# Scores of the second attention from two f16 halves of the context, which the first stage stores

## The reference, cut to what matters

```python
x = x + _L0_xattn_ref(ctx_1024, _layernorm(x), w_q, w_kv, w_out, b_out)      # 16 heads, keys and values from the context
x = x + _L0_ffn_ref(_layernorm(x), gate_w, gate_b, expert_w, expert_b)       # all 8 experts, weighted by counts
x = x + _L1_xattn_ref(_layernorm(x), ctx_1024, ctx_1024, mask)               # one head, context as keys and values
x = x + _L1_ffn_ref(_layernorm(x), W1, b1, W2, b2, Wg, bg)                   # the best 2 of 8 experts a token

def _L1_xattn_ref(q, k, v, mask):
    logits = jnp.einsum('bqd,bkd->bqk', q, k) * scale
    logits = logits + mask * NEG
    attn = jax.nn.softmax(logits, axis=-1)
    return jnp.einsum('bqk,bkd->bqd', attn, v)
```

## Time and profile before

| | us |
|---|---|
| median of three timed runs | 1064.37 (1064.32 to 1065.72) |
| profiled execution, its own time | 1060.8 |
| profiled execution, span from first to last instruction | 1059.0 |
| TensorE busy | 959.3 (91%) |
| VectorE busy | 763.2 (72%) |
| ScalarE busy | 552.9 (52%) |
| GpSimd busy | 564.6 (53%) |
| mean granted clock of TensorE, of full speed | 0.97 |

### The profile page before, as it was taken

The page is one execution under the profiler, slowest core; times in us unless marked ns, Lnnn a source line. Parts: engine busy times, 40 slices in busy tenths (PEclk is TensorE's granted clock), DMA queues, the critical chain, the costliest instruction groups (busy, mean ns, idle before and its releaser), DMA issues. The chain is left out here.

```text
span 1059.0 us, 31414 instructions
## 1 busy us (share of the span) xinstructions
PE 959.3 (91%) x10666; PEld 675.3 (64%) x10666; DVE 763.2 (72%) x2164; ACT 552.9 (52%) x1090; POOL 564.6 (53%) x904
## 2 busy tenths in 40 slices
PE   4799999999999999988799999999963699999993
PEld 2466666666666666656456666666642588888872
DVE  4688788887888888894768888888765266666553
ACT  3566666666666666655224444444442355555541
POOL 6655454555545555410126777777776355555444
PEclk9999999999999999998799999999997799999997
DMA  5644344444444344322355656555561355555443
GB/s 153 174 136 135 104 121 122 136 110 123 118 127 136 110 122 120 108 79 83 104 151 166 187 189 194 181 179 184 182 197 58 119 91 90 98 96 92 83 63 41
DMA packets 104687, 134.03 MB, mean 127 GB/s; under 512 B 23713, under 2 KB 93873, under 8 KB 104369
## 3 DMA queue, kind: packets, MB, share of 16 engines
q1 hardware_dynamic: 90994, 113.93, 36.6%
q0 software_dynamic: 13536, 18.10, 10.1%
HBM read 93.80 MB, written 38.73 MB: 125 GB/s over the span
## 5 line engine op out<-in xcount | busy, mean ns | idle before, releaser
L991 DVE TENSOR_REDUCE smax<-psum 112x2 f32<-112x750 f32 x240 | 221.2, 934 | 45.8 <-PE psum L443 44.5
L823 ACT ACTIVATE probsT<-psum 125x896 f32<-125x896 f32 x173 | 158.8, 918 | 54.7 <-PE psum L458 53.4
L1963 POOL DMA_INDIRECT out_dram<-y,token_at x70 | 111.9, 1599 | 112.0 <-DMA out_dram<-y,token_at 53.5
L2044 ACT ACTIVATE h<-psum,b 128x256 f32<-128x256 f32 x140 | 58.7, 470 | 99.5 <-PE psum L1991 99.5
L1718 DVE SCALAR_TENSOR_TENSOR acc<-psum,neg_bias,acc 128x448 f32<-128x448 f32 x112 | 75.8, 679 | 10.8 <-PE psum L1542 10.7
L443 PE MATMUL psum<-k_stack,q_stack 63*128 63x375 f16 x480 | 78.5, 326 | 3.5 <-DVE smax L991 0.7
L478 PE MATMUL psum<-probsT,v_aug 125*32 125x112 f32 x2688 | 81.6, 262 | 0.0
L1461 POOL DMA_INDIRECT dispatch_dram<-rows,slots_at x64 | 64.0, 1000 | 28.4 <-issue 28.4
L1542 PE MATMUL psum<-xT_hi,we_hi 128*128 128x448 f16 x256 | 70.2, 356 | 1.1 <-ACT we_hi L1640 1.1
L396 POOL CAST k_hi<-we 128x375 f16<-128x375 f32 x64 | 31.9, 498 | 73.6 <-ACT we L843 73.5
L458 PE MATMUL psum<-q_stack,k_stack 64*128 64x112 f16 x1384 | 64.2, 212 | 7.3 <-DMA q_stack<-neg_max 2.7
(11 more groups left out here) (277 smaller groups left out, 2455.6 us busy)
## 6 DMA issues: line engine op xcount, KB each, us to landing
k_stack<-k_hi_dram SPq DMA_DIRECT2D x64, 188.0 KB, 2.8
we<-in_ctxT_dram SPq DMA_DIRECT2D x32, 375.0 KB, 3.7
ctxT<-in_ctxT_dram SPq DMA_DIRECT2D x32, 375.0 KB
ctx_rows<-in_ctx_dram SPq DMA_DIRECT2D x32, 375.0 KB
rows_e<-dispatch_dram SPq DMA_DIRECT2D x70, 136.0 KB, 2.4
w_raw<-in_w_dram SPq DMA_DIRECT2D x32, 256.0 KB, 3.8
k_hi_dram<-k_hi SPq DMA_DIRECT2D x32, 188.0 KB, 3.2
k_lo_dram<-k_lo SPq DMA_DIRECT2D x32, 188.0 KB, 3.4
```

What stands on the lines that cost most here:

```text
L823: nc.scalar.activation(probsT[:, p, c, hg, :, :, :].rearrange("p k h q -> p k (h q)"), psum[0:KC, 0:2, 0:4 * S], ACT.Exp, scale=float(HD) ...
L991: nc.vector.reduce_max(smax[:, (u - LAG_B) % 2, 2 * (s % 4) + s // 4::PAIRS], psum[0:S, pair_bank(s):pair_bank(s) + 2, 0:KV], AX.X).then_i ...
L1963: nc.gpsimd.indirect_dma_start(dram["out"], bass.IndirectOffsetOnAxis(token_at[:, n % 2, s:s + 1], 0), y[:, n % 2, s, :], None, compute_op ...
L2044: nc.scalar.activation(h[:, c, :], psum[:, 1 + c // 2, (c % 2) * TILE:(c % 2 + 1) * TILE], ACT.Relu, bias=b1[:, c, bass.ds(e, 1)]).then_in ...
```

## The change

In the first stage SyncE gets `halves_out(b)`: two transfers that store `ctx_hi` and `ctx_lo` of batch b, 187.5 KB each, in a new tensor in device memory. It is called in step b behind the queries' rows into `q_stack` and ahead of the load or `q_hi` out; in step 2 it isn't called, and in step 3 for the batches 2 and 3. Two semaphores, `ctx_out0` and `ctx_out1`, count the stores of even and odd batches. `ctx_high` and `ctx_low` wait for those of the batch two before, whose slot they write, and SyncE for all of them before the next weights are loaded.

In the second stage the f32 load of the context becomes one load of both halves, of as many bytes. `x2nT` becomes `x2nT_hi`, by ScalarE ahead of the row normalisation instead of behind it, and `x2nT_lo`, a new subtraction on VectorE ahead of mixture 3. The scores are six f16 products instead of two f32 ones, and TensorE waits for `x2nT_lo` ahead of the last two. The turning of x3 moves from ahead of the ranks to behind them. Left out of the diff below: to make room for three new semaphores, `share_ps` is merged with `share_rdy`, `route_split` with `bias_rdy` and `pads_out` with `late_in`, each with its counts raised.

```diff
@@ -178,6 +178,7 @@
...
     MASK_AT = 2 * UNROLL
+    LATE_HALVES = 2
 
@@ -238,6 +239,13 @@
         @block.sync
         def _(sp):
+            def halves_out(b):
+
+                sp.wait_ge(m["ctxlo_ready"], b + 1)
+                apart(sp)
+                for n, half_of in enumerate((ctx_hi, ctx_lo)):
+                    sp.dma_start(dram["ctx_halves"][b, n, :, :], half_of[:, b % 2, :, :].rearrange("p c k -> p (c k)")).then_inc(m[f"ctx_out{b % 2}"], 16)
+
             def load(t, u):
@@ -287,6 +295,8 @@
...
                         part_in(sp, "q_" + QUERY_PARTS[part], u - 1, q_stack, part, q_in)
+                for b in {LATE_HALVES: (), LATE_HALVES + 1: (LATE_HALVES, LATE_HALVES + 1)}.get(t * UNROLL + u, (t * UNROLL + u,)):
+                    halves_out(b)
                 if 0 < t * UNROLL + u < UNROLL:
@@ -329,6 +339,8 @@
...
                         part_in(sp, "q_" + QUERY_PARTS[part], last, q_stack, part, q_in)
+            for n in range(2):
+                sp.wait_ge(m[f"ctx_out{n}"], 32 * B // 2)
             sp.wait_ge(m["mask_moved"], 16 + 1 + 16)
@@ -355,6 +367,7 @@
...
                 wait(pool, m["v_done"], count(t, u - 2, 2, 2))
+                wait(pool, m[f"ctx_out{u % 2}"], 2 * slot_loads(t, u - 2, 2))
                 nc.gpsimd.tensor_tensor(ctx_lo[:, u % 2, :, :], ctxT[:, u % 2, :, :], ctx_hi[:, u % 2, :, :], ALU.subtract).then_inc(m["ctxlo_ready"], 1)
@@ -827,6 +840,7 @@
...
                 wait(act, m["v_done"], count(t, u - 2, 2, 2))
+                wait(act, m[f"ctx_out{u % 2}"], 2 * slot_loads(t, u - 2, 2))
                 nc.scalar.activation(ctx_hi[:, u % 2, :, :], ctxT[:, u % 2, :, :], ACT.Copy).then_inc(m["ctxhi_ready"], 1)
@@ -1258,7 +1272,7 @@
...
 
-    ctxT = sb("ctxT2", [128, 2, DC, KV], F32)
+    ctx_halves = sb("ctx_halves", [128, 2, 2, DC, KV], F16)
     ctx_rows = sb("ctx_rows", [KC, 2, NKC, D], F32)
@@ -1267,7 +1281,7 @@
...
     x2n = sb("x2n", [S, D], F32)
-    x2nT = sb("x2nT", [128, DC, S], F32)
+    x2nT_hi, x2nT_lo = sb("x2nT_hi", [128, DC, S], F16), sb("x2nT_lo", [128, DC, S], F16)
     probs = sb("probs", [S, KV], F32)
@@ -1415,7 +1429,8 @@
...
                 apart(sp)
-                sp.dma_start(ctxT[:, p, :, :], dram["ctxT"][bass.ds(b, 1), :, :].rearrange("o (c p) s -> p (o c) s", p=128)).then_inc(ctxT_in[p], 16)
+                sp.dma_start(ctx_halves[:, p, :, :, :].rearrange("p n c k -> p n (c k)"),
+                             dram["ctx_halves"][b, :, :, :].rearrange("n p f -> p n f")).then_inc(ctxT_in[p], 16)
                 wait(sp, m["masked_rdy"], cnt(t, u - 2, 1, 1))
@@ -1583,12 +1597,6 @@
...
                 mix(3)
-                if r:
-                    wait(pe, m["x3n_rdy"], cnt(t, ur, 1, 1))
-                    wait(pe, m["lg_rdy"], cnt(t, ur - 1, 1, 1))
-                    for kc in range(DC):
-                        last = nc.tensor.transpose(psum[:, 7, kc * S:(kc + 1) * S], rows[:, ur % ROW_SLOTS, kc * 128:(kc + 1) * 128], ident[0:S, 0:S])
-                    last.then_inc(m["x3nT_done"], 1)
                 if k:
@@ -1600,17 +1608,28 @@
...
                     nc.tensor.matmul(rank, ones[:, 0:S], cum[:], start=False, stop=True).then_inc(m["rank_done"], 1)
+                if r:
+                    wait(pe, m["x3n_rdy"], cnt(t, ur, 1, 1))
+                    wait(pe, m["lg_rdy"], cnt(t, ur - 1, 1, 1))
+                    for kc in range(DC):
+                        last = nc.tensor.transpose(psum[:, 7, kc * S:(kc + 1) * S], rows[:, ur % ROW_SLOTS, kc * 128:(kc + 1) * 128], ident[0:S, 0:S])
+                    last.then_inc(m["x3nT_done"], 1)
                 if a:
...
                     wait(pe, m["masked_rdy"], cnt(t, ua - 1, 1, 1))
-                    for kc in range(DC):
-                        last = nc.tensor.matmul(psum[0:S, 4, 0:KV], x2nT[:, kc, :], ctxT[:, ua % 2, kc, :], start=(kc == 0), stop=(kc == DC - 1))
+                    n = 0
+                    for x, half_of in ((x2nT_hi, 0), (x2nT_hi, 1), (x2nT_lo, 0)):
+                        if n == 2 * DC:
+                            wait(pe, m["x2lo_rdy"], cnt(t, ua, 1, 1))
+                        for kc in range(DC):
+                            last = nc.tensor.matmul(psum[0:S, 4, 0:KV], x[:, kc, :], ctx_halves[:, ua % 2, half_of, kc, :], start=(n == 0), stop=(n == 5))
+                            n += 1
                     last.then_inc(m["s1_done"], 1)
...
                     if isinstance(t, int) and t * TURN + ur == 0:
-                        pe.wait_ge(m["route_split"], 2)
+                        pe.wait_ge(m["bias_rdy"], 4)
                     wait(pe, m["x3lo_rdy"], cnt(t, ur, 1, 1))
@@ -1665,6 +1684,10 @@
...
                     nc.scalar.activation(logit_exp[:], logits[:], ACT.Exp, bias=neg_top[:]).then_inc(m["lexp_rdy"], 1)
+                if a:
+                    wait(act, m["x2nT_done"], cnt(t, ua, 1, 1))
+                    wait(act, m["s1_done"], cnt(t, ua - 1, 1, 1))
+                    nc.scalar.activation(x2nT_hi[:].rearrange("p c s -> p (c s)"), psum[:, 2, D:D + DC * S], ACT.Copy).then_inc(m["x2nT_rdy"], 1)
                 if r:
@@ -1806,6 +1825,10 @@
...
                     nc.vector.scalar_tensor_tensor(x3[:, uo % 2, :], psum[0:S, 6, 0:D], inv_sum[:], xrow(uo), ALU.mult, ALU.add).then_inc(m["x3_rdy"], 1)
+                if a:
+                    wait(dve, m["x2nT_rdy"], cnt(t, ua, 1, 1))
+                    nc.vector.tensor_tensor(x2nT_lo[:].rearrange("p c s -> p (c s)"), psum[:, 2, D:D + DC * S],
+                                            x2nT_hi[:].rearrange("p c s -> p (c s)"), ALU.subtract).then_inc(m["x2lo_rdy"], 1)
                 if f:
@@ -2199,6 +2222,7 @@
...
         dram[name] = nc.dram_tensor(f"{name}_dram", (2, 128, DC * cols), F16, kind="Internal").ap()
+    dram["ctx_halves"] = nc.dram_tensor("ctx_halves_dram", (B, 2, 128, DC * KV), F16, kind="Internal").ap()
     dram["mask_scaled"] = nc.dram_tensor("mask_scaled_dram", (B, KV), F32, kind="Internal").ap()
```

More of the change, by code:

```diff
@@ L1400, in _ @@
             for n in range(2):
-                sp.dma_start(dram["dispatch"][DUMMY + n * 128:DUMMY + (n + 1) * 128, :], dram["pads"][n]).then_inc(m["pads_out"], 16)
+                sp.dma_start(dram["dispatch"][DUMMY + n * 128:DUMMY + (n + 1) * 128, :], dram["pads"][n]).then_inc(m["late_in"], 16)
             for n in range(3):
-                sp.dma_start(dram["out"][PAD_OUT + n * 128:PAD_OUT + (n + 1) * 128, :], dram["pads"][n][:, 0:D]).then_inc(m["pads_out"], 16)
+                sp.dma_start(dram["out"][PAD_OUT + n * 128:PAD_OUT + (n + 1) * 128, :], dram["pads"][n][:, 0:D]).then_inc(m["late_in"], 16)
             def store(t, u):
@@ L1526, in _ @@
                 last = nc.tensor.matmul(psum[:, 0, 0:E], ones[0:S, :], gate_counts[:, n, :], start=(n == 0), stop=(n == 4))
-            last.then_inc(m["share_ps"], 1)
-            pe.wait_ge(m["share_rdy"], 1)
+            last.then_inc(m["share_rdy"], 1)
+            pe.wait_ge(m["share_rdy"], 2)
             def mixture(t, u, k):
@@ L1634, in _ @@
         def _(act):
-            act.wait_ge(m["share_ps"], 1)
+            act.wait_ge(m["share_rdy"], 1)
             nc.scalar.activation(share[:], psum[:, 0, 0:E], ACT.Copy, scale=1.0 / (2 * B * S)).then_inc(m["share_rdy"], 1)
-            act.wait_ge(m["share_rdy"], 1)
+            act.wait_ge(m["share_rdy"], 2)
             for e in range(E):
@@ L1675, in step @@
                                          scale=ln_rstd[:, 1, :]).then_inc(m["x3n_rdy"], 1)
-                if a:
-                    wait(act, m["x2nT_done"], cnt(t, ua, 1, 1))
-                    wait(act, m["s1_done"], cnt(t, ua - 1, 1, 1))
-                    nc.scalar.activation(x2nT[:].rearrange("p c s -> p (c s)"), psum[:, 2, D:D + DC * S], ACT.Copy).then_inc(m["x2nT_rdy"], 1)
                 if r:
@@ L1750, in step @@
                     dve.wait_ge(m["weights_in"], 16 * N_W)
-                    nc.vector.tensor_copy(route_whi[:], route_w[:]).then_inc(m["route_split"], 1)
-                    dve.wait_ge(m["route_split"], 1)
-                    nc.vector.tensor_tensor(route_wlo[:], route_w[:], route_whi[:], ALU.subtract).then_inc(m["route_split"], 1)
+                    nc.vector.tensor_copy(route_whi[:], route_w[:]).then_inc(m["bias_rdy"], 1)
+                    dve.wait_ge(m["bias_rdy"], 3)
+                    nc.vector.tensor_tensor(route_wlo[:], route_w[:], route_whi[:], ALU.subtract).then_inc(m["bias_rdy"], 1)
                 if f:
```

13 lines of the change are left out of this document (6 added, 7 removed).

## The result

The changed kernel takes 1074.82 us (median of six runs, 1072.65 to 1076.79), the kernel before 1064.19: a ratio of 1.0111, 95% interval [1.0084, 1.0137]. The profiled execution has a time of 1074.89 us, its span is 1072.7 us, 13.7 above the span of before. The prediction said 1066.7 and 1061.0 to 1071.5. The direction was right; the size is outside the range.

A forecast was written before the change was run, and what follows sets the result against it. TensorE, busy 91% of the span, was taken to bound the kernel. First stage +11.4 and second stage -9.1 gave +2.3 us on the timed 1064.37: 1066.7 us, range 1061 to 1071.5.

The forecast's parts named there:

- First stage: Attention over the context: +11.4 us, from the stage's start, where ScalarE's new wait for held-back stores is not hidden.
- the release: First stage, step 3: the third batch's stores free ScalarE's fifth ctx_high at 51.3 us, landing 3.4 us after issue.
- the 0.8 us of delay on SyncE's queue: First stage's start: the second batch's stores delay SyncE and its queue by 0.8 us, bounds 0 and 1.5.
- The first exponential: ScalarE behind the stalled ctx_high in the first stage: at 52.35 instead of 42.94 us, +9.4, bounds +8 and +11.
- the predicted 2: First stage's start: TensorE's idling lowers its granted clock to 1.2 GHz, costing +2.0 us, bounds 0 and +3.5.
- The steady steps: First stage behind its start: added stores and ScalarE's wait are hidden, 0 us, bounds 0 and +3.
- The step's gain: Second stage, each step with all parts: f16 scores save 0.29 us on TensorE, bounds 0.20 and 0.36.
- 8.1 were forecast for the loop: Second stage ahead of draining: 7.5 us from 26 full steps and 0.6 from two steps before routing starts.
- 0.28 is left. ... Hidden.: Second stage, VectorE: 0.87 us of waits cover 0.30 for x2nT_lo and 0.29 of shorter step, so the subtraction costs nothing.
- The prediction's own chain: Second stage: transposes, xT_hi and xT_lo end at 656.65, scores at 656.58, so TensorE waits 0.07 us before routing.
- VectorE becomes the bound: Second-stage rival: x2nT_lo pushes xT_lo back 0.15 us a step, 3.9 us comes back, 1070.6 us; chance 0.12.
- drain and third stage, -1.0 and 0 in the sum: Second stage's four draining steps gain 0.25 us each, -1.0 in all; 0 for everything behind them.

The follow-up runs named there:

- e1: Changed kernel with the second stage's f32 scores put back, keeping the first stage's stores and their waits: 1072.77 us, ratio 1.0079 to the kernel before.
- e3: Changed kernel with no batch held back, every batch's halves stored in its own step: 1063.83 us, ratio 1.0009 to the kernel before.
- e2: Changed kernel with each batch's stores moved behind the previous step's k_lo and none held back: 1062.15 us, ratio 0.9983 to the kernel before.
- e13: e5 with two small operations, exp_bias and neg_top, moved from VectorE to ScalarE: 1061.63 us, ratio 0.9985 to the kernel before.
- e4: Changed kernel without the per-step x2nT_lo subtraction on VectorE (set to zero once): 1070.38 us, ratio 1.0063 to the kernel before.
- e8: The changed kernel run once more, unchanged: 1074.18 us, ratio 1.0105 to the kernel before.
- e7: e5's store places, with the second stage's scores in f32 as before the change: 1063.72 us, ratio 1.0004 to the kernel before.
- e14: e11 without its last 22 idle products on TensorE: 1062.73 us, ratio 0.9982 to the kernel before.
- e15: e13 and e14 together: 1056.9 us, ratio 0.9948 to the kernel before.
- e11: e5 with idle products on TensorE in the draining steps and the waits up to the third stage: 1066.04 us, ratio 1.0008 to the kernel before.
- e5: e2 with the fourth batch's stores behind the first maxima's row instead of ahead of it: 1063.54 us, ratio 0.9999 to the kernel before.
- e9: e5 with GpSimd's w_lo subtraction ahead of the two scatters instead of behind them: 1079.0 us, ratio 1.0137 to the kernel before.

## Why the prediction was wrong

**First stage: the mechanism right, 3 us too dear.** The wait, its place, what is queued behind it and the half clock came as written. Of the terms, the release was 49.30, not 51.3: the 0.8 us of delay on SyncE's queue didn't come (the keys' rows of step 3 start at 41.92, before at 42.50), and a store of this kind lands 2.7 us after its issue (part 6 of the page), not 3.4, the row that I took it from. The first exponential is 50.39, +7.5 instead of +9.4. With the clock the stage was 9.3 behind by the next maxima (61.2 against 51.9), so the clock took the predicted 2. The steady steps cost nothing, as predicted (14.71 us before, 14.72 after); by the masked maxima it is +8.3, and by e1's ratio 8.4.

**The step's gain: right for an undisturbed step, but few were.** 0.29 was forecast and 0.22 is what e3 shows. The scores with their wait take 1.04 where 1.33 stood, a gain of 0.29, to the hundredth; 0.02 go in the transposes ahead (0.22 to 0.23 instead of 0.20) and 0.05 in the routing products behind (0.33 to the next operation instead of 0.28). 27 x 0.22 = 5.9, where 8.1 were forecast for the loop.

**The first step that failed: "0.28 is left. ... Hidden."** I counted VectorE's slack, got it right (8.27 - 8.01 = 0.26), and took an amount above zero for enough. It is enough only if nothing ever comes late. Before, VectorE had 0.87 us of waits a step and its late starts, 3 in 26 steps, drowned in them: TensorE's steps were 8.49 throughout. xT_lo was ready 0.42 us ahead of its routing product. Now it is ready 0.05 ahead of it in every step, so whatever delays it delays TensorE. The prediction's own chain had this (xT_lo at 656.65, scores through at 656.58), and weighed VectorE's slack without it. VectorE can make up some 0.2 us between the masked maxima and xT_lo: in the change starts of 0.48 and 0.51 behind the routing product (0.2 later than usual) cost nothing, those of 0.56 to 0.71 make xT_lo late, and TensorE waits 0.13 us or more. The rival "VectorE becomes the bound" named the place and the price (0.15 a step; the profile shows 0.10: 5.9 were to be gained in 27 steps, 3.1 were, and 2.8 / 27 = 0.10); it had a chance of 0.12. Of the 2.8, 1.2 us are lost in e2 and e3 too, which have one late start each (loop 223.8 instead of 228.5 - 5.9 = 222.6); 1.6 go with the ten late starts. e13 shows the cause by removing it with the late starts still there; e4 points the same way, but takes late starts away as well; e8 shows that the cost repeats. That there are many more late starts than before is shown; why is open.

**The second and larger one: drain and third stage, -1.0 and 0 in the sum.** The profile has +3.9 and +4.5. The prediction took 0.25 us off each draining step, and for all that comes behind the loop it had no term and gave no reason: no step of it spoke of the clock there. In before TensorE's idle time was long already (22.02 us busy of 32.10).

How much of the +8.4 is the second stage's? Profiles of two executions differ here by themselves: the three with f32 scores have drains of 32.1, 34.7 and 34.7 and rests of 259.2, 258.4 and 261.3 us, those with f16 scores and no filling drains from 31.9 to 37.1 and rests from 261.2 to 265.0. On the mean the three have 33.8 and 259.6, the ten others 34.5 and 262.9. So the drain isn't shown to be longer at all (0.7), the rest is by 3.2, and together some 4.0 us of the +8.4 are the second stage's. I put what is left down to the two executions compared. Of the 3.2, 2.4 come behind the third stage's first expert product, whose program was not changed.

The clock is part of it. Half clock is 9 us longer on the mean with f16 scores, worth 0.6 to 2.5 us (e7, e14, e15). e11 shows that the clock follows TensorE's idle time: with filling the drain runs at 1.00. What the rest of the 4.0 us is stays open.

**The sum by the experiments.** By the ratio the change costs 11.8 us (8.9 to 14.6), where +2.3 was forecast. Start +8.4 (e1) instead of +11.4. Undisturbed steps -5.9 instead of -8.1, long steps +2.8 instead of 0, drain and what is behind it +4.0 instead of -1.0. These sum to +9.3; the 2.5 us that are missing lie within the ratio's interval. Without the start's stall the second stage gives -0.5 +- 2.5 us (e5 against e7) instead of -9.1, where the same terms with e5's long steps (5.9 - 2.1 = 3.8) sum to +1.9. Behind the stall it gives about +3 +- 4 (the change and e8 against e1). Whether the stall makes the second stage dearer is not resolved.

## What to carry to other kernels

When a bound engine is made faster, the slack of the next engine is what the gain is to be weighed against, and it has to cover that engine's irregular delays, not only its mean: look in the trace for idle times that are longer than usual every few steps, and count the steps in which they no longer fit. A wait that is added to free a buffer is priced by the store's place in its queue, and moving that store can be free: here the place alone was worth 8 us with the f32 scores (e1 against e7) and 10 to 14 with the f16 ones (the change against e3, e5 and e2). Give every stage behind the change a term, even where its program isn't touched: here the largest miss was a stretch that had none. And look at the granted clock where the bound engine idles, at the ends and starts of stages.

## What the runs showed of the hardware that was not expected

- With the f16 scores VectorE's masked maxima start 0.31 us behind the routing product in an undisturbed step, and in some steps 0.45 to 0.86 behind it, with no operation on VectorE between. How often the long distance comes (1 to 13 of 26) differs between kernels that differ only in the order of a few transfers 500 us earlier (e2, e3 against e5), differs again where only what follows the loop does (e11, e14: 10 and 9), and nearly repeats for the same kernel (10 and 11, e8). The cause wasn't found.
- An operation of 8 columns with two SBUF inputs lasted 1.24 us instead of 0.17 beside a subtraction of 1.16 us on GpSimd (e9).
- Idle products raised the granted clock of the drain from 0.78 to 1.00 and shortened it from 34.6 to 30.9 us (e11).
- Within each kernel an execution with one microsecond more of half clock was 0.27 us longer, about half of the 0.5 us that it would cost (an estimate from the two levels) if TensorE bound the kernel throughout. Taking half clock away by filling brought only 0.06 to 0.10 us for each microsecond (e14, e15).
